# Which dimension lies on the partitions in the expert outputs that are kept, and which engine brings them back

## What is computed

```python
topk_s, topk_i = jax.lax.top_k(scores, TOP_K)
w = jax.nn.softmax(topk_s, axis=-1)
out = jnp.zeros_like(x)
for ei in range(NUM_EXPERTS):
    g = jnp.where(topk_i == ei, w, 0.0).sum(-1)
    hh = jax.nn.gelu(x @ W1[ei] + b1[ei], approximate=False)
    out = out + g[..., None] * (hh @ W2[ei] + b2[ei])
return out
```

## Time and profile before

| | us |
|---|---|
| the kernel before, runs | 9057.4, 9059.58, 9065.71 |
| median of the runs | 9059.58 |
| profiled execution, its time | 9063.45 |
| profiled execution, span of the trace | 9061.7 |
| granted clock, mean over the span | 0.665 |

### The profile page before, as it was taken

How to read it: one execution, slowest core, us unless ns; L and a number is a source line. 1 busy time by engine, 2 the same in 40 slices (tenths; PEclk the granted TensorE clock), 3 DMA queues, 4 the chain that set the end, 5 groups by cost and what they waited for, 6 DMA issues and landing times. The chain is left out here.

```text
span 9061.7 us, 45970 instructions
## 1 busy us (share of the span) xinstructions
PE 3468.2 (38%) x9579; PEld 1623.4 (18%) x9579; DVE 3847.0 (42%) x7333; ACT 1987.3 (22%) x3855; POOL 5361.6 (59%) x4840
## 2 busy tenths in 40 slices
PE   7888498990003222222222222222222222222134
PEld 4555244440001001101010010101010011010001
DVE  7888798889532212121212122222222121212388
ACT  6777255550001111111111111111111111111011
POOL 4555000000467777777777777777777777777552
PEclk8888699995556666666666666666566666666555
DMA  3433222220011111111111111111111111111165
GB/s 104 125 118 116 70 99 76 82 83 21 7 28 43 32 44 32 44 32 44 34 42 37 39 40 36 44 32 44 32 44 32 44 32 44 32 44 32 51 217 202
DMA packets 344241, 532.42 MB, mean 59 GB/s; under 512 B 159307, under 2 KB 236026, under 8 KB 319098
## 3 DMA queue, kind: packets, MB, share of 16 engines
q1 hardware_dynamic: 196514, 473.73, 15.0%
q0 software_dynamic: 147552, 56.95, 5.4%
HBM read 299.88 MB, written 230.45 MB: 59 GB/s over the span
## 5 line engine op out<-in xcount | busy, mean ns | idle before, releaser
L1100 POOL DMA_INDIRECT e_got<-rows,e_index x4352 | 4601.4, 1057 | 1466.4 <-issue 1466.4
L1552 PE MATMUL ex_y_ps<-ex_hh,w_w 128*128 128x512 f32 x1024 | 948.5, 1082 | 4156.3 <-issue 2027.0
L1587 DVE SCALAR_TENSOR_TENSOR ex_z<-ex_y_ps,w_b,ex_gate 128x512 f32<-128x512 f32 x192 | 144.1, 751 | 3288.1 <-remote 1961.6
L1552 PEld LDWEIGHTS ex_y_ps<-ex_hh,w_w 128*128 128x128 f32 x1024 | 299.4, 322 | 4636.8 <-issue 3480.4
L1570 ACT ACTIVATE ex_hh<-ex_hid_ps,w_b 128x512 f32<-128x512 f32 x512 | 323.5, 683 | 2707.0 <-issue 1525.6
L942 POOL MEMSET q_word<- 128x128 int16 x1 | 0.2, 204 | 1150.4 <-POOLq L88 1150.4
L1534 PE MATMUL ex_hid_ps<-ex_tn,w_w 128*128 128x512 f32 x1024 | 619.3, 737 | 83.5 <-DMA ex_tn<-norm 61.2
L1191 DVE TENSOR_TENSOR_SCAN e_out<-e_near,e_out,e_wgt 128x64 f32<-128x64 f32 x1088 | 348.6, 365 | 509.5 <-issue 487.2
L493 PE MATMUL o_hid_ps<-o_tn,w_w 128*128 128x512 f32 x1024 | 524.6, 594 | 71.9 <-DMA o_tn<-norm 71.9
L506 PE MATMUL o_y_ps<-o_hh,w_w 128*128 128x512 f32 x1024 | 525.2, 595 | 14.7 <-ACT o_hh L524 14.7
L524 ACT ACTIVATE o_hh<-o_hid_ps,w_b 128x512 f32<-128x512 f32 x512 | 350.8, 687 | 366.5 <-PE o_hid_ps L493 366.5
(11 more groups left out here) (364 smaller groups left out, 5997.5 us busy)
## 6 DMA issues: line engine op xcount, KB each, us to landing
e_got<-rows,e_index POOLq DMA_INDIRECT x4352
kept<-o_kept SPq DMA_DIRECT2D x64, 1024.0 KB, 4.5
ex_gate<-gate SPq DMA_DIRECT2D x64, 1024.0 KB
c_kept<-kept SPq DMA_DIRECT2D x64, 1024.0 KB
sums<-e_out SPq DMA_DIRECT2D x68, 768.0 KB
m_xin<-in_x_dram SPq DMA_DIRECT2D x64, 512.0 KB, 4.7
mid<-m_xm SPq DMA_DIRECT2D x64, 512.0 KB, 2.9
norm<-m_tn SPq DMA_DIRECT2D x64, 512.0 KB, 5.0
```

Source lines behind the costliest of these rows:

```text
L1100: pool.indirect_dma_start(got[:, at % 2, c, :], None, rows_d, bass.IndirectOffsetOnAxis(ap=index[:, at % 2, c:c+1], axis=0)).then_inc(S["g ...
L1552: last = pe.matmul(self.y_ps[:, :], self.weights.w2[:, e, f, :], self.hh[:, e % 2 * HID + f, :], start=(f == 0), stop=(f == HID - 1))
```

## The change

`Outputs` makes `y` with tokens on the partitions: for each block of 128 tokens, `hh` of the block is the stationary and the 128 columns of `w2` are moving, four matmuls a gap in place of one. The bias now differs from column to column, so a bf16 matmul of 512 columns (ones times the bias, which is split in three bf16 parts on three partitions) starts each expert's sum in PSUM, and `keep` is a plain copy. The parts are made by eight DVE operations in `start_vector`; a DMA of `b2` goes ahead of the weight loads, and POOL does two memsets.

In `finish_lower` the gate of a token is then a per-partition scalar. `GateRows` goes, the gates are written in one f32 copy in place of the 7 operations, ACT copies a tile's 16 gate columns (`now`) and scales the first expert's four blocks into `acc`, and DVE adds the other three experts in 12 operations of 128 columns (`scalar_tensor_tensor`: kept times gate plus `acc`). PE adds `mid` by a matmul with the identity (512 columns) and turns the four blocks of `acc` with matmuls against the identity into the same PSUM bank; ACT brings the sum out into `o`. Loads into a slot wait for `turned` (set by PE), and the stores of a turn stand behind the next turn's loads and wait for `fin` (set by ACT). The second group peels four turns off its loop in place of two.

```diff
+        flat = self.weights.io["b2"].rearrange("(a e) c -> a (e c)", a=1)
+        sp.dma_start(self.b2[:, :], flat.broadcast_to([P, EXPERTS * P])).then_inc(self.S["b2d"], 16)
         self.weights.sync(sp, self.S["w"])
     def start_gpsimd(self, pool):
-        pass
+        pool.memset(self.ones[:, :], 1.0)
+        pool.memset(self.bias[:, :, :, :], 0.0).then_inc(self.S["zero"], 1)
     def start_tensor(self, pe):
...
+        S, n = self.S, [0]
+        def go(i):
+            n[0] += 1
+            i.then_inc(S["part"], 1)
+            v.wait_ge(S["part"], n[0])
+        v.wait_ge(S["b2d"], 16)
+        v.wait_ge(S["zero"], 1)
+        for i in range(PARTS):
+            go(v.tensor_copy(self.b2_part[:, i, :], self.b2[:, :]))
+            if i < PARTS - 1:
+                go(v.tensor_tensor(self.b2[:, :], self.b2[:, :], self.b2_part[:, i, :], ALU.subtract))
+        for i in range(PARTS):
+            one = slice(32 * i, 32 * i + 1)
+            part = self.b2_part[one, i, :].rearrange("p (e c) -> p e c", c=P).unsqueeze(2).broadcast_to([1, EXPERTS, BLKS, P])
+            go(v.tensor_copy(self.bias[one, :, :, :], part))
...
-                pe.matmul(self.y_ps[:, e % 2, :], self.weights.w2[:, e, f, :], self.hh[:, g % 2, :], start=(f == 0), stop=(f == HID - 1)).then_inc(S["y"], 1)
+                y = self.y_ps[:, e % 2, :]
+                if f == 0:
+                    if g == 0:
+                        pe.wait_ge(S["part"], 3 * PARTS - 1)
+                    pe.matmul(y, self.ones[:, :], self.bias[:, e, :, :].rearrange("p b c -> p (b c)"), start=True, stop=False)
+                for b in range(BLKS):
+                    last_y = pe.matmul(y[:, b*P:(b+1)*P], self.hh[:, g % 2, b*P:(b+1)*P], self.weights.w2[:, e, f, :], start=False, stop=(f == HID - 1 and b == BLKS - 1))
+                last_y.then_inc(S["y"], 1)
...
-        act.activation(self.kept[:, r % 2, e, :], self.y_ps[:, e % 2, :], ACT.Identity, bias=self.weights.b2[:, e:e+1]).then_inc(self.S["kept"], 1)
+        act.activation(self.kept[:, r % 2, e, :], self.y_ps[:, e % 2, :], ACT.Copy).then_inc(self.S["kept"], 1)
...
-class GateRows:
...
-        weights = Gates(nc, ctx, io, S, "c", PER * GROUP, True)
-        rows = GateRows(nc, sb, ps, S, parts)
-        mask = sb("mask", [G, 8])
+        weights = Gates(nc, ctx, io, S, "c", PER * GROUP, False)
+        ident = sb("ident", [P, P])
...
-        kept = sb("kept", [P, 4, EXPERTS, TOK]); xm = sb("xm", [P, 4, TOK]); o = sb("o", [P, 4, TOK])
-        weighed = sb("weighed", [P, 2, EXPERTS, TOK]); pairs = sb("pairs", [P, 2, TOK]); total = sb("total", [P, TOK])
-        gate_ps = ps("gate_ps", [P, EXPERTS, TOK])
-        def gathered(k): return not isinstance(k, int) or k < TURNS
+        kept = sb("kept", [P, 4, EXPERTS, BLKS, P]); xm = sb("xm", [P, 4, TOK]); o = sb("o", [P, 4, TOK])
+        gate = sb("gate", [P, HIS * EXPERTS]); now = sb("now", [P, 4, EXPERTS * BLKS]); acc = sb("acc", [P, 4, BLKS, P])
+        out_ps = ps("out_ps", [P, 2, TOK])
         def turns(eng, group, body):
 
             first = GROUP * group
-            peeled = (GROUP, 2, 0, 0, 0)[group] if group < 4 else 0
+            peeled = (GROUP, 4, 0, 0, 0)[group]
...
+                def store(k, at):
+                    for t, u, j in tiles(k, at):
+                        sp.wait_ge(S["fin"], t + 1)
+                        sp.dma_start(out_d[k - GROUP, :, j*TOK:(j+1)*TOK], o[:, u, :]).then_inc(S["st%d" % u], 16)
...
-                        need(sp, S["fin"], t + 1)
-                        sp.dma_start(out_d[k - GROUP, :, j*TOK:(j+1)*TOK], o[:, u, :]).then_inc(S["st%d" % u], 16)
-                        load(t + 4, k - GROUP + 2, u, j)
...
+                        sp.wait_ge(S["turned"], t + 1)
+                        load(k - GROUP + 2, u, j, t + 4)
+                    if follows(k):
+                        store(k - 1, 1 - at)
...
-                        need(pe, S["gst"], t + 1)
-                        need(pe, S["gt"], t)
-                        pe.sem_inc(S["go"], 1)
-                        rows.turn(pe, rows.turned_ps, j).then_inc(S["gtp"], 1)
-                        need(pe, S["gt"], t + 1)
-                        for e in range(EXPERTS):
-                            need(pe, S["mul"], (t - 1) * EXPERTS + e + 1)
-                            pe.matmul(gate_ps[:, e, :], rows.choose[:, e, :], rows.turned[:, j, :], start=True, stop=True).then_inc(S["sel"], 1)
+                        pe.wait_ge(S["sum"], ADDS * (t + 1))
+                        need(pe, S["fin"], t - 1)
+                        pe.sem_inc(S["free"], 1)
+                        pe.matmul(out_ps[:, j, :], ident[:, :], xm[:, u, :], start=True, stop=False)
+                        for b in range(BLKS):
+                            last = pe.matmul(out_ps[:, j, b*P:(b+1)*P], acc[:, u, b, :], ident[:, :], start=False, stop=(b == BLKS - 1))
+                        last.then_inc(S["turned"], 1)
...
+                def scale(k, at, pair):
+                    for t, u, j in tiles(k, at):
+                        need(act, S["turned"], t - 3)
+                        act.activation(now[:, u, :], gate[:, bass.ds(t * (EXPERTS * BLKS), EXPERTS * BLKS)], ACT.Copy).then_inc(S["now"], 1)
+                        act.wait_ge(S["ld%d" % u], 32 * (pair - GROUP // 2 + 1))
+                        act.wait_ge(S["now"], t + 1)
+                        for b in range(BLKS):
+                            last = act.activation(acc[:, u, b, :], kept[:, u, 0, b, :], ACT.Copy, scale=now[:, u, b:b+1])
+                        last.then_inc(S["scaled"], 1)
+                def evict(k, at, pair):
+                    for t, u, j in tiles(k, at):
+                        act.wait_ge(S["turned"], t + 1)
+                        need(act, S["st%d" % u], 16 * (pair - GROUP // 2))
+                        act.activation(o[:, u, :], out_ps[:, j, :], ACT.Copy).then_inc(S["fin"], 1)
                 def body(k, at, pair):
-                    for t, u, j in tiles(k, at):
-                        need(act, S["gtp"], t - 1)
-                        act.activation(rows.staged[:, j, :, :], parts[:, bass.ds(t * BLKS, BLKS), :], ACT.Identity).then_inc(S["gst"], 1)
-                        need(act, S["gtp"], t + 1)
-                        need(act, S["sel"], (t - 1) * EXPERTS)
-                        act.activation(rows.turned[:, j, :], rows.turned_ps[0:G, 0:TOK], ACT.Identity).then_inc(S["gt"], 1)
+                    scale(k, at, pair)
+                    if follows(k):
+                        evict(k - 1, 1 - at, pair - 1 + at)
...
-                rows.start_vector(v, go, mask)
-                assert n[0] == 15
...
-                        v.wait_ge(S["ld%d" % u], 32 * (pair - GROUP // 2 + 1))
-                        need(v, S["sum"], 3 * (t - 1))
-                        for e in range(EXPERTS):
-                            need(v, S["sel"], t * EXPERTS + e + 1)
-                            v.tensor_tensor(weighed[:, j, e, :], kept[:, u, e, :], gate_ps[:, e, :], ALU.mult).then_inc(S["mul"], 1)
-                        need(v, S["mul"], t * EXPERTS + EXPERTS)
-                        need(v, S["fin"], t)
-                        v.tensor_tensor(pairs[:, 0:2, :], weighed[:, j, 0:2, :], weighed[:, j, 2:4, :], ALU.add).then_inc(S["sum"], 1)
-                        need(v, S["sum"], 3 * t + 1)
-                        v.tensor_tensor(total[:, :], pairs[:, 0, :], pairs[:, 1, :], ALU.add).then_inc(S["sum"], 2)
-                        need(v, S["sum"], 3 * t + 3)
-                        need(v, S["st%d" % u], 16 * (pair - GROUP // 2))
-                        v.tensor_tensor(o[:, u, :], total[:, :], xm[:, u, :], ALU.add).then_inc(S["fin"], 1)
+                        v.wait_ge(S["scaled"], t + 1)
+                        for e in range(1, EXPERTS):
+                            for b in range(BLKS):
+                                if e > 1:
+                                    v.wait_ge(S["sum"], t * ADDS + (e - 2) * BLKS + b + 1)
+                                n = e * BLKS + b
+                                v.scalar_tensor_tensor(out=acc[:, u, b, :], in0=kept[:, u, e, b, :], scalar=now[:, u, n:n+1], in1=acc[:, u, b, :],
+                                                       op0=ALU.mult, op1=ALU.add).then_inc(S["sum"], 1)
...
-                        weights.vector(v, group, agg[:, cols, :], parts[:, cols, :])
+                        weights.vector(v, group, agg[:, cols, :], gate[:, PER*GROUP*EXPERTS*group:PER*GROUP*EXPERTS*(group+1)])
```

More of the change, by code:

```diff
@@ L1637, in finish_lower @@
-def finish_lower(nc, io, mid_d, out_d, kept_d, res_d, agg, parts, pos_i, gathers):
+def finish_lower(nc, io, mid_d, out_d, kept_d, res_d, agg, pos_i, gathers):
     PER, TURNS, GROUP = 2 * BLKS, HIS // (2 * BLKS), 8
+    ADDS = (EXPERTS - 1) * BLKS
     with ExitStack() as ctx:
@@ L1666, in tiles, with follows @@
             return [(k * 2 - 2 * GROUP + j, 2 * at + j, j) for j in range(2)]
+        def follows(k):
```

(6 more changed lines are left out.)

65 lines of the change are left out of this document (14 added, 51 removed).

## The result

| | before | after |
|---|---|---|
| median of the runs, us | 9061.07 (5 runs, 9057.4 to 9065.71) | 9112.56 (5 runs, 9107.57 to 9117.58) |
| ratio, 95% interval | | 1.0057 (1.0042 to 1.0071) |
| span of the profiled execution, us | 9061.7 | 9110.8 |

The kernel became 51 us slower, where the prediction said 31 us faster and a range up to 9088. Cut at the same events in both traces, the stages say where. The gates of a group begin with the first operation on `agg` and end with the last write of a gate; a group lies between the end of one group's gates and the start of the next one's.

A forecast was written before the change was run, and what follows sets the result against it. PE was taken to set the sort's pace, DVE to be busy some 88 us of each gather group. Terms 3 + 47.7 - 3.9 - 9.2 - 58.4 - 10.2 = -31 gave 9029 us; own range 9008 to 9055, with rivals 8993 to 9088.

The forecast's parts named there:

- Sort: Second stage: small matmuls and bias add 0.137 us a gap in 491 gaps, less PE's 19.6 us first wait: +47.7 us.
- first block: Start of the sort: DVE's eight bias operations cost 6.4 us, less 3.2 of cover in its wait for POOL's iota: +3.
- Start: Start of `finish_lower`: POOL's first gather no longer waits 3.97 us for the index copy behind 15 small operations: -3.9 us.
- gates: Gates of the four groups in `finish_lower`: one copy replaces 2.7 us of splits on DVE, 4 x 2.3: -9.2 us.
- Three groups: Groups with gathers and weighing in `finish_lower`: POOL's gathers set the pace, three groups take 242 us: -58.4 us.
- price of a gather: POOL in the three groups: 1.075 us a gather plus 0.30 between, 11.0 us a turn of 8 gathers.
- R1: Rival: DVE's two-operand operations slow every gather to 1.38 us; the groups give 7 us instead of 58; 9080 us, chance 0.15.
- forecast of 81 us a group: Three groups in `finish_lower`: seven turns of POOL's gathers back to back, 77 + 3.6 = 80.6 us each.
- Last group: End of `finish_lower`, without gathers: a chain of loads at 336 GB/s takes 76.2 us in place of 86.4: -10.2 us.
- R2: Rival in the sort: small matmuls miss their 0.110 us a record; 9088 us at 0.125, 9449 at full unhidden load; chance 0.14.
- R4: Rival in the groups: at 0.4 us a small operation DVE stays the bound, 10.4 us a turn; within the forecast's range.
- R3: Rival, more gain: gathers stay at 0.945 us (-22) and small-matmul records at 0.107 (-12): 8995 us, chance 0.11.

## Why the prediction was wrong

**Sort, right.** +52.5 us to its end, predicted 50.7. The small matmuls had their price of 0.110 (0.111 measured), the bias 0.21 a matmul (0.23 taken), the first stall gave its 19.6, and the added time behind the fourteenth crossing disappeared. The prediction had from the Trainium skill (TensorE: Matmul & The Clock Gate, section "The mechanism") that a weight load overlaps a matmul only where the row groups differ; that is not borne out here, as each record has a full-height load of its own and eight of them take 0.89 us, where columns alone would be 0.86, and the section's other case, a load into the background weight buffer, would fit. The first block's +3.7 is near the forecast's +3 by luck. POOL's iota was no free cover: the first cast, begun beside it, took 3.74 us and ended 0.28 us after it, where the second took 0.43.

```profile
1002.14 3.55 POOL L618 IOTA s_dst<- 128x4096 int32 x1 [46.75 <-DVEq L670]
1002.23 3.74 DVE L479 CAST o_b_part<-o_b 128x512 bf16<-128x512 f32 x1 [0.22 <-DVE s_ping L656]
...
1006.73 0.43 DVE L479 CAST o_b_part<-o_b 128x512 bf16<-128x512 f32 x1
```

From the end of the operation before the iota to the copy of the iota it is 5.2 us more than before. But the iota began 1.5 us earlier in this execution, and the three copies were cheaper than taken (2.12 us together, not 3.45).

**Start, gates, right.** -3.8 and -9.1.

**Three groups, wrong: the step that failed is the price of a gather, 1.075 us.** I took it from a mean (1.03) and raised it a little, because there are more operations with two SBUF operands. But it doesn't go by their share of the time. A gather that meets such an operation waits for its end and then needs 0.82 us more; with single operations of 1.2 us at most that made 1.42 at the worst in the groups (the forecast took 1.38 for the worst), and the mean hid it. When 24 such operations follow without a gap, the wait is for the rest of the chain: one gather a turn of 4.8 us in the mean, 93 us in all, of which 22 were in my price. So some 71 of the 90 are these. The rest is about 10 for seven more gathers in the groups than the 168 of the sum, and 9 for two waits of POOL for its indices (4.75 and 5.12 us). R1 named the right pair of engines and the right direction and still priced it at 51 us, because it, too, gave each gather the 1.38 of the single operation. The Trainium skill (GPSIMD Engine Reference, section "1. Specifications") names contention at an interface to SBUF that POOL and VectorE share, when a VectorE operation has two SBUF inputs; the runs agree in the condition (with one operand in PSUM the 4.2 to 5.5 us of the held gathers become 0.96 at most in the groups), and they add the size for a chain, which no row of before could give. The interface itself no run shows.

**And the forecast of 81 us a group was out of reach without the hold, too.** DVE's 3.2 us a tile, ACT, PE and the DMA were about right: without gathers the groups are 64 to 72 us. This is the second step that failed, the overlap: gathers back to back beside the other engines' work. Gathers that follow each other without a hold keep the other engines from going on; with the hold gone, the groups still took 98 to 106. In the kernel before, DVE set the pace and POOL mostly paused after eight gathers; 36 of its 38 slow instructions stand beside its only two longer trains (15 gathers with eight more close behind, 8656 to 8687, and 23, 8888 to 8918). The kernel after had 1, though its gathers follow each other for up to 64; that the held gather stood for a pause there is argued, not shown. So the 58 us that I had set on "POOL back to back" would have been 0 to 19 even without the hold (301.2 before; 301.6 with loops, 282.1 without).

**Last group, right mechanism, size off by 12.** Cut at the gates it was 92.8 before, not 86.4, so I had left out 6.4 us at its two ends. Most of the rest is the rate of the transfers: I took 336 GB/s, and in the 48 us in which they run in full it was 396, where PE ran at 0.89 of its clock and not the 0.50 of the earlier trace rows.

```profile
9052.00:9100.00 48.00, 28.05 (x122) 18.88 (x121) 38.44 (x145) 22.44 (x73) 0.00 (x0) 0.89 1.02 396
```

**R2** (small matmuls) and **R4** (DVE stays the bound) fell: 0.111 us a record, and an addition every 0.263 us. **R3** (gathers at 0.945) fell with the held gathers.

## What to carry to other kernels

When a change puts one engine's operations into a chain without gaps, look in the trace before for what another engine's instructions wait for at the *end* of such an operation (a constant distance between two ends, here 0.82 us, is the sign), and price the wait by the length of the new chain, not by the mean of the old rows. An operand in PSUM instead of SBUF took the hold away at no cost to DVE (an addition every 0.258 us in place of 0.263). A forecast that makes another engine "run back to back" is a forecast of a state that the trace has not shown: bound it by a stretch in which it did, with the same work beside it.

## What was not expected of the hardware

- A gather held by DVE gets on only at the end of the chain, and not at the borders between its operations. Those that begin in the chain's first 1.6 us pass, and from 1.73 us on they are held but for one. The border isn't sharp: in the kernel without the bias in the sort, with the same finish, one begun 1.47 us into its chain was held and one begun at 2.05 passed. Why the start of a chain is open wasn't tried.
- It goes the other way round, too: DVE's cast of 512 columns beside POOL's iota ended 0.28 us after the iota, in 3.74 us in place of 0.43. It did so in the kernel after and in each of the nine runs that keep this block.
- Beside trains of gathers, register instructions of SP and DVE took 0.70 us in place of 0.04. In code without them single engines stood still, ACT for 10.8 us in the rows above, and PE, ACT and DVE together for 3 to 4 us; with the bias added by tile it was up to 14 us together. It needs no loops, and a quarter of the loads doesn't end it. With trains of eight, pauses of 1.2 us didn't prevent it (50 slow instructions), and those of about 2.8 us halved it (25). But in the kernel before, 2 slow instructions stand beside its trains of eight, with pauses of mostly 1.1 to 1.6 us, so the length of the pause alone doesn't decide. What the engines lack there stays open.
- The granted clock in the finish was 0.68 to 0.84 after the change, 0.50 before, with PE's busy time about the same in the groups with gathers (43 to 46 us), now in f32 matmuls.
